# Four-layer graph network on one core: sorted edges scattered in three stages, the last layer's lists loaded a stage earlier

## The reference

```
L0: out = segment_sum(norm * x[col], row) @ W.T + b              # norm from node degrees
L1: 4 heads of 32: softmax over the edges of a node of leaky_relu(q[src].k[dst]), times v[src]
L2: twice: agg = segment_sum(x[src]*ew, dst) + x
           out = leaky(x @ Ws.T + bs + (agg/cnt) @ Wn.T + bn + bias);  then @ W_agg.T + b_agg
L3: xw = x @ W;  out = segment_sum(xw[src] * (edge_attr @ edge_w), dst) + b
```

## Time and profile before

| | us |
| --- | --- |
| median of 3 runs | 3131.64 (3122.51 to 3140.24) |
| the profiled execution | 3137.08 |
| its span, first to last instruction | 3135.3 |
| PE busy | 2324.6 (74%) |
| DVE busy | 1929.2 (62%) |
| POOL busy | 1985.7 (63%) |
| ACT busy | 1301.7 (42%) |

### The profile page before, as it was taken

How to read it: one execution, slowest core, us unless ns; L and a number is a source line. 1 busy time by engine, 2 the same in 40 slices (tenths; PEclk the granted TensorE clock), 3 DMA queues, 4 the chain that set the end, 5 groups by cost and what they waited for, 6 DMA issues and landing times. The chain is left out here.

```text
span 3135.3 us, 63975 instructions
## 1 busy us (share of the span) xinstructions
PE 2324.6 (74%) x22192; PEld 1705.1 (54%) x22192; DVE 1929.2 (62%) x3807; ACT 1301.7 (42%) x2282; POOL 1985.7 (63%) x1608
## 2 busy tenths in 40 slices
PE   3667677750039578787777788798993799999998
PEld 2466666640014245555555555553542587877776
DVE  7999999960023577777777777721112465656564
ACT  0466666650000377777777777500001222222221
POOL 2378878787772388788888888300000488887885
PEclk6799998875569679989999999999996799999998
DMA  6266666661146111111111111199692322222222
GB/s 77 95 168 188 185 185 180 186 186 15 11 99 160 59 48 46 42 45 42 45 45 45 45 44 41 39 228 221 140 213 9 66 55 61 55 56 55 54 56 56
DMA packets 219167, 285.61 MB, mean 91 GB/s; under 512 B 130289, under 2 KB 163960, under 8 KB 215725
## 3 DMA queue, kind: packets, MB, share of 16 engines
q1 hardware_dynamic: 170258, 246.53, 31.5%
q0 software_dynamic: 48720, 36.84, 6.2%
HBM read 171.50 MB, written 112.09 MB: 90 GB/s over the span
## 5 line engine op out<-in xcount | busy, mean ns | idle before, releaser
L385 POOL DMA_INDIRECT scratch_slots<-sort_pay,sort_slot x400 | 630.8, 1577 | 171.5 <-issue 171.2
L1796 POOL TENSOR_TENSOR score<-score,rise 125x500 f32<-125x500 f32 (+1 forms) x609 | 671.6, 1137 | 47.8 <-DVE peaks L1732 43.8
L2334 POOL DMA_INDIRECT gathered_rows<-scratch_projected,src_i x425 | 524.3, 1234 | 195.2 <-issue 194.6
L1732 DVE CUSTOM_DVE_ANT_0 score<-raw,log_in 125x500 f32<-125x500 f32 (+1 forms) x609 | 354.7, 619 | 151.9 <-PE raw L1617 87.8
L1679 ACT ACTIVATE rise<-raw 125x1000 f32<-125x1000 f32 (+1 forms) x350 | 314.3, 917 | 165.0 <-DVE peaks L1732 83.5
L1632 PE MATMUL probsT<-ident,score 125*125 125x125 f32 x2175 | 358.4, 294 | 29.8 <-ACT score L1688 13.1
L1632 PEld LDWEIGHTS probsT<-ident,score 125*125 125x125 f32 x2175 | 298.3, 200 | 106.8 <-DVE weighed L1753 67.0
L843 PE MATMUL built<-pair_weight,hot 125*128 125x125 bf16 x3750 | 265.5, 237 | 107.6 <-DVE pair_weight L790 107.6
L843 PEld LDWEIGHTS built<-pair_weight,hot 125*128 125x128 bf16 x3750 | 243.5, 107 | 123.7 <-DVE pair_weight L790 123.7
L790 DVE TENSOR_TENSOR pair_weight<-hot,w_parts 125x3840 bf16<-125x3840 bf16 x125 | 270.7, 2165 | 17.2
L1617 PE MATMUL raw<-QT,key 32*125 32x500 f32 (+1 forms) x1400 | 200.1, 642 | 93.3 <-DVE peaks L1732 90.2
(11 more groups left out here) (304 smaller groups left out, 4392.3 us busy)
## 6 DMA issues: line engine op xcount, KB each, us to landing
weights_in<-scratch_weightsT SPq DMA_DIRECT2D x50, 1093.8 KB
scratch_weightsT<-wT SPq DMA_DIRECT2D x25, 1367.2 KB
scratch_logs<-log SPq DMA_DIRECT2D x75, 437.5 KB
log_in<-scratch_logs SPq DMA_DIRECT2D x150, 218.8 KB
counts_in<-scratch_counts SPq DMA_DIRECT2D x25, 683.6 KB
scratch_counts<-cc SPq DMA_DIRECT2D x24, 683.6 KB
gathered_rows<-scratch_projected,src_i POOLq DMA_INDIRECT x425, 3.4
scratch_slots<-sort_pay,sort_slot POOLq DMA_INDIRECT x400
```

The costliest lines, as they stand in the source:

```text
L385: nc.gpsimd.indirect_dma_start(rows, bass.IndirectOffsetOnAxis(ap=sort["slot"][:, b, c:c + 1], axis=0), pay[:, c, :], None).then_inc(sort[ ...
L1732: nc.vector.tensor_tensor_reduce(out=score[u][h][:, at:at + w], in0=raw[:, h, 0:w], in1=log_in[:, at:at + w], scale=1.0, scalar=-3e38, op0 ...
L1796: nc.gpsimd.tensor_tensor(score[u][h][:, at:at + w], score[u][h][:, at:at + w], rise[:, b, h, 0:w], ALU.add).then_inc(added, 1)
L2334: nc.gpsimd.indirect_dma_start(gathered[:, g % GATHERS, k, :], None, projected, bass.IndirectOffsetOnAxis(ap=src_i[:, FIRST + g, k:k + 1], ...
```

## The change

Three things are moved.

- `adjacency` places five blocks, L0 one, and `weighted_layers` four, through a new `place_blocks` that issues the first attribute load of its stage itself. The buffers `sort_raw` and `sort_pay` are made anew in each stage; the slot numbers stay in memory until then.
- `fetch_last_layer` issues, on SP at the end of `attention`, `base_i`, the last 85 groups of `src_i` and `dst_i`, and the nine weight loads. The zero fills move to `one_over_degree`, where POOL also clears the semaphores of the branch for irregular graphs (15).
- The first 80 groups of `src_i` and `dst_i` are loaded by SP at the end of the second block of `edge_layer`, which waits for them. DVE converts and shifts `dst_rel` for the 85 groups alone.

```
+GATHERED = SORTED // (EG * P)
+PLACED_IN_ADJACENCY = 5
+PLACED_IN_FIRST_LAYER = 1
+PLACED_EARLY = PLACED_IN_ADJACENCY + PLACED_IN_FIRST_LAYER
...
+def place_blocks(nc, T, pool, sort, slots, first, end):
+    nc.gpsimd.dma_start(sort["raw"][:], attribute_block(T, first)).then_inc(sort["raw_in"], 16)
+    for b in range(first, end):
+        place_block(nc, T, pool, sort, slots, b, end)
+    wait_placed(pool, sort, end)
...
 # place_block
-    if b + 1 < SORT_BLOCKS:
+    if b + 1 < end:
         nc.gpsimd.dma_start(sort["raw"][:], attribute_block(T, b + 1)).then_inc(sort["raw_in"], 16)
...
 # adjacency, POOL
             for b in range(PLACED_IN_ADJACENCY):
-                place_block(nc, T, pool, sort, slots, b)
+                place_block(nc, T, pool, sort, slots, b, PLACED_IN_ADJACENCY)
...
 # regular_gcn_layer, POOL
-            for b in range(PLACED_IN_ADJACENCY, SORT_BLOCKS):
-                place_block(nc, T, pool, sort, slots, b)
-            wait_placed(pool, sort, SORT_BLOCKS)
+            place_blocks(nc, T, pool, sort, slots, PLACED_IN_ADJACENCY, PLACED_EARLY)
...
 # weighted_layers, POOL
+            place_blocks(nc, T, pool, sort, slots, PLACED_EARLY, SORT_BLOCKS)
...
 # one_over_degree
+            clear_used(pool, left)
+            nc.gpsimd.memset(last["mix"][:], 0.0)
+            nc.gpsimd.memset(last["quad_mix"][:], 0.0)
...
+def fetch_last_layer(nc, T, sp, last):
+        sp.dma_start(last["base_i"][:], T["dst"].rearrange("(o g r) -> o g r", o=1, r=EG * P)[:, :, 0]).then_inc(last["in"], 16)
+        for name, out in (("src", last["src_i"]), ("dst", last["dst_i"])):
+            sp.dma_start(out[:, GATHERED:, :], T[name][SORTED:].rearrange("(g p c) -> p g c", p=P, c=EG)).then_inc(last["in"], 16)
+    for k in range(EG):
+        sp.dma_start(last["mix"][k * EDIM:(k + 1) * EDIM, k, :], T["L3_gnn_edge_w"]).then_inc(last["in"], 16)
+    for k in range(4):
+        sp.dma_start(last["quad_mix"][k * SLOT:k * SLOT + EDIM, k, :], T["L3_gnn_edge_w"]).then_inc(last["in"], 16)
...
 # edge_layer, second block, end of SP's stream
+                    for name, out in (("src", src_i), ("dst", dst_i)):
+                        sp.dma_start(out[:, 0:GATHERED, :], T[name][0:SORTED].rearrange("(g p c) -> p g c", p=P, c=EG)
+                                     ).then_inc(last["in"], 16)
+                sp.wait_ge(last["in"], 16 * (LAST_LOADS + 2))
```

More of the change, by code:

```diff
@@ L971, in general_adjacency @@
     STEPS = CHUNKS // STEP
+    own = []
     with ExitStack() as c:
@@ L1132, in gcn_layer @@
         last = e(nc.psum_tensor(unique("last_bank"), [P, 512], F32))
[L1133 to L1142, removed]
+        loaded = [sem(f"loaded{u}") for u in range(BUFS)]
+        used = sem("used")
+        scaled_done = sem("scaled_done")
+        bias_done = sem("bias_done")
+        agg_moved = sem("agg_moved")
+        inv_done = sem("inv_done")
+        root_ready = sem("root_ready")
+        root_done = sem("root_done")
+        lin_done = sem("lin_done")
+        lin_added = sem("lin_added")
+        slot_buffers(nc, e, sort)
         block = e(nc.Block())
@@ L1467, in _, with attention @@
             sp.wait_ge(keys_stored, 16)
-def attention(nc, logs, keysT, X, H, QT, V, ident):
+def fetch_last_layer(nc, T, sp, last):
+    with nc.allow_non_contiguous_dma(reason="runs of five edges, and one destination of every group"):
+        sp.dma_start(last["base_i"][:], T["dst"].rearrange("(o g r) -> o g r", o=1, r=EG * P)[:, :, 0]).then_inc(last["in"], 16)
[5 more added lines that the diff above has]
+        sp.dma_start(last["quad_mix"][k * SLOT:k * SLOT + EDIM, k, :], T["L3_gnn_edge_w"]).then_inc(last["in"], 16)
+LAST_LOADS = 3 + EG + 4
+def attention(nc, T, logs, keysT, X, H, QT, V, ident, last):
     PW = 4 * P
@@ L1801, in attention, with one_over_degree, _ @@
     return used
-def one_over_degree(nc, in_parts, per_node):
+def one_over_degree(nc, in_parts, per_node, last, left):
     with nc.semaphore(unique("degree_done")) as degree_done, nc.Block() as block:
+        @block.gpsimd
+        def _(pool):
+            clear_used(pool, left)
+            nc.gpsimd.memset(last["mix"][:], 0.0)
+            nc.gpsimd.memset(last["quad_mix"][:], 0.0)
         @block.vector
@@ L2111, in edge_layer @@
     QROWS = QUAD * SLOT
-    assert FIRST * EDGES == SORTED and LISTS % 2 == 0
+    assert FIRST * EDGES == SORTED and FIRST == GATHERED and LISTS % 2 == 0
+    base_i, src_i, dst_i, mix, quad_mix = [last[k] for k in ("base_i", "src_i", "dst_i", "mix", "quad_mix")]
     with ExitStack() as c:
@@ L2181, in _ @@
             def _(sp):
-                with nc.allow_non_contiguous_dma(reason="runs of five edges, and one destination of every group"):
-                    sp.dma_start(base_i[:], T["dst"].rearrange("(o g r) -> o g r", o=1, r=EDGES)[:, :, 0]).then_inc(edges_in, 16)
-                    sp.dma_start(src_i[:], T["src"].rearrange("(g p c) -> p g c", p=P, c=EG)).then_inc(edges_in, 16)
-                    sp.dma_start(dst_i[:], T["dst"].rearrange("(g p c) -> p g c", p=P, c=EG)).then_inc(edges_in, 16)
-                sp.wait_ge(mix_zero, 2)
-                for k in range(EG):
-                    sp.dma_start(mix[k * EDIM:(k + 1) * EDIM, k, :], T["L3_gnn_edge_w"]).then_inc(attr_in, 16)
-                for k in range(QUAD):
-                    sp.dma_start(quad_mix[k * SLOT:k * SLOT + EDIM, k, :], T["L3_gnn_edge_w"]).then_inc(attr_in, 16)
                 sp.wait_ge(copied, len(quads()))
@@ L2327, in _ @@
                 assert b == SORT_BLOCKS
+                with nc.allow_non_contiguous_dma(reason="runs of five edges"):
+                    for name, out in (("src", src_i), ("dst", dst_i)):
+                        sp.dma_start(out[:, 0:GATHERED, :], T[name][0:SORTED].rearrange("(g p c) -> p g c", p=P, c=EG)
+                                     ).then_inc(last["in"], 16)
+                sp.wait_ge(last["in"], 16 * (LAST_LOADS + 2))
             @block.gpsimd
@@ L2633, in program @@
+        one_over_degree(nc, in_parts, per_node, last, left)
         with ExitStack() as heads:
@@ L2639, in program @@
                 project(nc, HT, W, QT, keysT, V)
-            used = attention(nc, logs, keysT, X, H, QT, V, ident)
+            used = attention(nc, T, logs, keysT, X, H, QT, V, ident, last)
         with sb("HT", [D, LISTS * DEPTH]) as HT:
```

89 lines of the change are left out of this document (45 added, 44 removed).

## The result

| | before | after |
| --- | --- | --- |
| median, us | 3135.94 (3122.51 to 3145.19, 4 runs) | 2900.56 (2899.66 to 2910.59, 4 runs) |
| the profiled execution's span, us | 3135.3 | 2898.9 |
| mean granted clock of PE | 0.875 | 0.906 |

The changed kernel takes 0.926 of the time, with a 95% interval of 0.9218 to 0.9301. The forecast was 2901.5 us, between 2880 and 2945.

A forecast was written before the change was run, and what follows sets the result against it. POOL working alone at the adjacency's end, then PE idle at the last layer's start, were taken as the bounds. Terms -194.2 + 1.0 + 8 + 1.1 - 46.0 = -230.1 gave a median of 2901.5 us, range 2880 to 2945.

The forecast's parts named there:

- The adjacency: End of adjacency: with nine blocks cut to five, POOL is no longer last and its excess goes, -194.2 us.
- a faster rest: Adjacency: DVE, ACT and PE speeding up with fewer scatters beside them; taken as nothing.
- L0 and `one_over_degree`: First layer: one block with its load requested later, +1.0 us; then POOL's clears and fills, +1.1 us.
- The four blocks, POOL's side: Weighted layers: four blocks at 67.7 us plus first load, 281 us, fit in 322; POOL ends 41 us early.
- Rival (a): Weighted layers: POOL becomes the end of the stage, at the adjacency's pace +84 us, 2986 us; chance 0.12.
- (d): Weighted layers: scatters wait out weights packets, 4.2 us each, stage 360 us late, 3262 us; chance 0.02.
- The four blocks, the weights' side: Weighted layers: scatters and attribute loads delay the weights PE waits for, +8 us, between 0 and 19.
- a DMA microsecond is a PE microsecond: Weighted layers, saturated first half: DMA time taken by 2.05 blocks delays PE equally, 9.6 us.
- rival (b): Weighted layers: the weights suffer more, +20 us in place of +8, 2914 us, up to 2925; chance 0.08.
- Lists at the end of attention: Early loads cost 0 in attention and remove PE's idle time at the last layer's start, -46.0 us.
- The store of `xw_rows`: Start of last layer: next possible late item, landing within 13 us against an 18.7 us list chain; still hidden.
- The late lists: End of last layer's main block: two late loads need 24.6 us, land 12 us early; cost 0, up to +12.

The follow-up runs named there:

- lists_only: Changed kernel with its early lists, mixing weights and fills, but blocks placed nine, one and none as before: 3087.83 us, 0.9857 of the kernel before.
- split613: Changed kernel with six blocks in the adjacency, one in the first layer, three in the weighted layers: 2908.71 us, 0.9313 of the kernel before.
- late613: Changed kernel with six, one and three blocks, POOL held in the weighted layers until PE used 20 of 70 weight slices: 2908.19 us, 0.9288.
- all_lists: Changed kernel with all 165 groups of both lists loaded at the end of attention, none late: 2913.99 us, 0.9308 of the kernel before.

## Why the prediction was right, step by step

**The adjacency.** POOL is no longer last: right. The size was 7.0 us short, in the term that I put at nothing, a faster rest. DVE's last step began at 685.90 instead of 688.34, and SyncE issued its last store at 698.50 instead of 705.22. The two rows are from the changed kernel's timelines of DVE and of SyncE's queue.

```profile
685.90 1.30 DVE L821 TENSOR_REDUCE out_degree<-degree_parts 125x25 f32<-125x625 f32 x1 [0.22 <-ACT degree_parts L884]
```

```profile
698.50 0.40 SPq L117 DMA_DIRECT2D scratch_logs<-log  x1
```

Of the 6.7 us at the last store 0.7 are the shorter preparation, which is the run's own, and 1.8 lie in the work up to DVE's last step. The other 4.3 lie behind it: from DVE's last step to SyncE's last store it is 16.9 us before and 12.6 here. That tail is 12.2 to 12.9 us in all ten profiles whose scatters had ended by then, with one to five blocks, and 16.0 to 16.9 us in the four that scatter beside it (before, lists_only, split613, late613). So fewer scatters beside the last stores are the cause of some 4 us. Here are the same two rows in split613, whose scatters last until 698.23:

```profile
682.22 1.31 DVE L821 TENSOR_REDUCE out_degree<-degree_parts 125x25 f32<-125x625 f32 x1 [0.22 <-ACT degree_parts L884]
...
698.36 0.40 SPq L117 DMA_DIRECT2D scratch_logs<-log  x1
```

**L0 and `one_over_degree`.** +1.0 and +0.9 against +1.0 and +1.1. POOL awaited the attribute load for 3.24 us, where I had allowed 10, and nobody waited for POOL.

**The four blocks, POOL's side.** The choice of the first layer's pace over the adjacency's was right: 67.7 us per block in the earlier trace rows and 68.0 us here. POOL ended 55.6 us before the stage and not 41, mostly since the stage got 11.8 us longer. Rival (a) is out, and so is (d), which needed 3.4 us per scatter. The Trainium skill, "DMA: Bandwidth & Descriptors", section "Queues, rings and completion order", has each engine finish a whole packet before it turns to another queue row; by my estimate from it the 160 scatters would have taken up to 480 us. They took 272, under a DMA share of 1.05 in the first 122 us, and the last of their packets had moved 6.6 us after the last issue. The trace doesn't bear that estimate out for this mix of queues; whether the rule fails here or my taking a packet of the trace for a descriptor of the page, no run shows.

**The four blocks, the weights' side.** Here the step was mis-sized. I wrote that a DMA microsecond is a PE microsecond, for 2.05 blocks of 4.7 us: 9.6, taken as +8, at most 19. The first profile had +11.8; over all profiles it is 15.9, and by medians 23 to 26. So this term came out nearer to the +20 of rival (b). Two things were missing. PE's waits grew by 11.6 us, more than the 9.6 that the shares give: the first of them came 45 to 55 us after the stage's start in the five profiles with four blocks, 68 to 76 us after it in the four without. And the products themselves took 4.1 us more. PE's clock was 0.96 in this window of the changed kernel, some of its worst 40 us (columns as above), and 1.00 in the same part of before (its 221 GB/s window above).

```profile
1923.00:1963.00 40.00, 32.81 (x86) 14.74 (x85) 4.18 (x10) 0.64 (x2) 31.92 (x27) 0.96 1.03 218
```

The clock is no sufficient cause. In the same 40 us all_lists, with the blocks, was granted 1.00, and lists_only, without them, 0.96:

```profile
1922.00:1962.00 40.00, 31.52 (x87) 14.32 (x87) 4.19 (x10) 0.64 (x2) 31.78 (x28) 1.00 1.03 219
```

```profile
2122.00:2162.00 40.00, 35.87 (x106) 17.07 (x105) 6.33 (x17) 0.64 (x2) 0.00 (x0) 0.96 1.04 222
```

Over the whole stage the mean clock is 0.984 with four blocks and 0.989 without. By my estimate from these two that is 1.4 of the 4.1 us; what lengthened the products beyond it stays open.

The DMA queues of the changed kernel from 1843 to 2178, beside the 3.3 us per block that I took from the earlier trace rows: 6.1% of 335 us is 20.4 us for four, 5.1 per block with its attribute load, against my 4.7. The load on the engines was sized right; what it does to PE was not.

```profile
q1 hardware_dynamic: 25764, 60.58, 84.0%
q0 software_dynamic: 5440, 2.91, 6.1%
```

**Lists at the end of attention.** -44.8 against -46.0, and 43.5 by the medians of lists_only. The store of `xw_rows` stayed hidden, as the prediction had it. The 12 issues took 32 us of SyncE's queue; its two longest in the changed kernel's timeline:

```profile
1751.84 12.78 SPq L1501 DMA_DIRECT2D dst_i<-in_dst  x1
1764.67 15.88 SPq L1503 DMA_DIRECT2D mix<-in_L_gnn_edge_w  x5
```

**The late lists.** Cost 0, right, with 7 us to spare where I had 12: they need 31.1 us, not 24.6. The rate of 1.23 us per thousand packets was read where no gathers ran; beside the gathers it is 1.54. All eleven profiles with late loads kept 4.6 to 8.0 us.

**The attention.** I had no term for it, and none was missing. The same 998 us are 988 to 1006 in the fourteen profiles, and the difference goes with the clock that PE is granted. These are the windows of the stage in the changed kernel, twice; columns as above.

```profile
828.28:1821.65 993.37, 770.16 (x9028) 529.20 (x9028) 749.25 (x2097) 728.93 (x840) 769.53 (x700) 0.92 0.17 44
```

```profile
828.38:1832.55 1004.17, 783.95 (x9028) 539.21 (x9028) 746.88 (x2097) 729.62 (x840) 769.69 (x700) 0.90 0.17 43
```

**The median.** 2900.56 lies 0.9 us from the forecast, and that is luck in part. The terms were off by -7.0, +3.8, -4.8, +1.2 and +0.7, together -6.4 with the small ones, which put the profiled execution at 2900.6 instead of 2907.0; and it lay on its own median, not 5.4 above it as in before. Two of these errors, the attention's clock and a part of the adjacency's, are the run's own, and they hid that the weights' term was 8 us too small by the mean of the profiles and up to 18 by the medians. The later set of the same kernel gave 2915.37. The range of 2880 to 2945 holds both.

## What to carry to other kernels

Where one engine alone works ahead of a barrier, its excess over the next engine is the gain to be had, and the cover for the moved work is found by reading that engine's pace under the same neighbours, here 68 us per block in the two layers, where DVE is busy for less than half of the time, and 95 to 105 beside the adjacency's work. The price is then paid by whoever waits on the shared DMA engines, and it came out at two to three times the forecast; that such work costs less behind the stretch in which the consumer waits is likely and not shown. A stage of a single profile is good to some us only, so a term of that size needs several profiles before it is explained, and its start must be counted from a mark close by: here a load in the preparation moved everything behind it by up to 5.5 us.

## What the runs showed of the hardware

- The same 60.6 MB of weights came at 221 to 247 GB/s in the same 40 us of the stage in four profiles with no blocks beside them, and PE's waits for them went from 2.5 to 12.8 us.
- PE's granted clock over the attention was 0.89 to 0.92, and its length 988 to 1006 us, for identical work.
- Scatters of 125 rows of 72 bytes kept their pace of 1.48 us against a DMA share of 1.05, for 160 to 200 of them in blocks of 40.
- SyncE issued the last of its stores in the adjacency 12.2 to 12.9 us after DVE's last step without such scatters beside them, and 16.0 to 16.9 us after it with them.
- Loads of 20-byte runs cost 1.23 us per thousand alone and 1.54 beside indirect gathers.
